# Zero rows of the first attention's stacks: two transfers in place of Pool's clearings, and a wait for each group of weights

## What is computed

```
c_q = x @ w_dq.T;   q_c = (c_q @ w_uq.T)        # 16 heads x 16
c_kv = x @ w_dkv.T; k_c = (c_kv @ w_uk.T); v = (c_kv @ w_uv.T)
q_r = (c_q @ w_qr.T); k_r = (x @ w_kr.T)        # 16 heads x 64
q_r, k_r = _rope(q_r, k_r, offset=0)
q = concatenate([q_c, q_r]); k = concatenate([k_c, k_r])
attn = softmax(q @ k.T * SCALE + causal mask); out = (attn @ v) @ w_out.T
```

## Time and profile before

| | us |
|---|---|
| median of 3 runs | 918.64 |
| lowest and highest of them | 917.73, 919.67 |
| the profiled execution | 916.41 |
| its span on the core | 914.2 |
| PE busy in the span | 791.1 (87%) |
| DVE busy | 365.2 (40%) |
| ACT busy | 290.5 (32%) |
| Pool busy | 224.3 (25%) |

### The profile page before, as it was taken

How to read it: one execution, slowest core, us unless ns; L and a number is a source line. 1 busy time by engine, 2 the same in 40 slices (tenths; PEclk the granted TensorE clock), 3 DMA queues, 4 the chain that set the end, 5 groups by cost and what they waited for, 6 DMA issues and landing times.

```text
span 914.2 us, 14814 instructions
## 1 busy us (share of the span) xinstructions
PE 791.1 (87%) x5020; PEld 602.4 (66%) x5021; DVE 365.2 (40%) x902; ACT 290.5 (32%) x527; POOL 224.3 (25%) x260
## 2 busy tenths in 40 slices
PE   1989799999989999999955289989887999999990
PEld 0767577877767677777734257767665767777760
DVE  8444154543533312222146386676543422222212
ACT  1102103114233333433223214445453234334321
POOL 8341013333131411221123300011312421221212
PEclk9999899999999999999986789999998999999995
DMA  6963914223962216110221641211301111101004
GB/s 198 409 142 107 315 67 93 59 48 89 360 207 74 70 55 207 40 35 23 63 78 32 177 103 34 56 45 35 142 30 53 58 36 34 34 24 34 29 18 143
DMA packets 47692, 88.19 MB, mean 96 GB/s; under 512 B 8884, under 2 KB 36916, under 8 KB 45524
## 3 DMA queue, kind: packets, MB, share of 16 engines
q1 hardware_dynamic: 36104, 54.56, 21.0%
q0 software_dynamic: 7568, 30.97, 9.3%
q10 hardware_dynamic: 3968, 1.97, 0.8%
HBM read 52.33 MB, written 35.13 MB: 96 GB/s over the span
## 4 chain that ended last, share of the span: by engine, by line
PE 80%; DVE 8%; DMA 6%; issue 2%; ACT 2%; POOL 1%; SPq 0%; ACTq 0%; POOLq 0%; DVEq 0%
PE bank L1380 24%; PE bank L1407 13%; PE bank L880 9%; PE bank L459 4%; PE bank L504 4%; PE bank L1393 4%; PE bank L515 2%; PE bank L449 2%; PE bank L533 2%; PE bank L502 2%; PE bank L576 2%; DMA PTR<-rows_out 2%; DVE stat L324 2%; DVE XN L596 1%; PE bank L550 1%
## 5 line engine op out<-in xcount | busy, mean ns | idle before, releaser
L1380 PE MATMUL bank<-wgu,R 128*128 x736 | 225.4, 459 | 0.4 <-issue 0.3
L1380 PEld LDWEIGHTS bank<-wgu,R 128*128 128x128 f32 x736 | 137.7, 193 | 65.8 <-issue 3.5
L1407 PE MATMUL bank<-R 112*128 (+1 forms) x552 | 127.0, 379 | 1.2 <-ACT R L1429 1.2
L1407 PEld LDWEIGHTS bank<-R 112*128 112x128 f32 (+1 forms) x552 | 104.4, 190 | 22.3 <-issue 1.7
L1445 DVE TENSOR_TENSOR R<-R,bank 128x344 f32<-128x344 f32 x92 | 47.2, 513 | 179.9 <-PE bank L1380 172.2
L647 ACT ACTIVATE PTR<-bank 128x512 f32<-128x512 f32 x144 | 83.5, 597 | 97.7 <-PE bank L504 82.2
L1356 POOL DMA_INDIRECT rows_out<-R,XN x46 | 46.0, 999 | 169.4 <-ACT R L1437 157.7
L1452 DVE COPY R<-bank 112x512 f32<-112x512 f32 x46 | 31.7, 690 | 103.7 <-PE bank L1393 103.7
L596 DVE TENSOR_REDUCE XN<-bank 128x2 f32<-128x512 f32 x96 | 63.1, 684 | 10.7 <-PE bank L459 10.7
L1423 ACT ACTIVATE R<-bank 128x344 f32<-128x344 f32 x92 | 41.9, 457 | 76.4 <-PE bank L1380 76.2
L1437 ACT ACTIVATE R<-bank 128x256 f32<-128x256 f32 x46 | 17.7, 384 | 146.7 <-PE bank L1407 146.7
(11 more groups left out here) (167 smaller groups left out, 1292.0 us busy)
## 6 DMA issues: line engine op xcount, KB each, us to landing
wgu<-in_wgu SPq DMA_DIRECT2D x10, 1376.0 KB, 11.4
slots_in<-PTR POOLq DMA_DIRECT2D x1, 9088.0 KB, 26.1
row_of_slot<-in_unused POOLq DMA_DIRECT2D x2, 4544.0 KB, 17.6
R<-slots_in SPq DMA_DIRECT2D x46, 128.0 KB, 2.0
wgu<-R SPq DMA_DIRECT2D x32, 128.0 KB, 2.4
R<-R SPq DMA_DIRECT2D x32, 128.0 KB, 2.4
PTR<-rows_out SPq DMA_DIRECT2D x16, 256.0 KB, 3.1
R<-in_wd SPq DMA_DIRECT2D x8, 448.0 KB, 5.8
```

The source lines that it names most:

```text
L1380: last = nc.tensor.matmul(BK[2 * half + gu][:, 0:IH], xsT[:, p, kk, :], wgu[:, bass.ds(e * (KD * GU) + (kk * GU + gu * I + half * IH), IH) ...
L1407: last = nc.tensor.matmul(down_bank(i)[:, 0:D], hT[0:CH[c], p, c, :], wd[0:CH[c], bass.ds(e * (6 * D) + c * D, D)], start=c == 0, stop=c == 5)
```

## The change

The clearings of the stacks by Pool go. In their place Pool issues two transfers (one for each pair of stacks) that copy zeros from PTR into rows 16 to 31; rows 0 to 15 are no longer cleared, since the placements write them. Pool issues them when wuq, wuk and wuv have landed (s_wu), waits until both have landed (s_slots), waits for wqr and woa, and then issues the fill. SP waits for the two transfers in place of Pool's clearings before it places. The single wait of PE for six weights becomes three: wkr before items 2 to 5, the three of s_wu before 6 to 8, wqr and woa before 9 to 12. Two pairs of x loads share a semaphore each, so DVE waits for both loads of a pair.

```diff
-        s_x = [sem(f"s_x{b}") for b in range(B)]
+        s_x = [sem("s_x01"), sem("s_x23")]
+        s_wk = sem("s_wk")
+        s_wu = sem("s_wu")
...
-        INIT = 5
+        INIT = 3
...
-            for dst, src in ((wkr, "wkr"), (wuq, "wuq"), (wuk, "wuk"), (wuv, "wuv"), (wqr, "wqr"), (woa, "woa")):
+            sp.dma_start(wkr, dr["wkr"]).then_inc(s_wk, 16)
+            for dst, src in ((wuq, "wuq"), (wuk, "wuk"), (wuv, "wuv")):
+                sp.dma_start(dst, dr[src]).then_inc(s_wu, 16)
+            for dst, src in ((wqr, "wqr"), (woa, "woa")):
                 sp.dma_start(dst, dr[src]).then_inc(s_wc, 16)
-            sp.wait_ge(s_init, INIT)
+            sp.wait_ge(s_slots, 16 * 2)
...
-            pool.memset(R1[0:32, 0:2 * HA * S], 0.0).then_inc(s_init, 1)
-            pool.memset(room(EVEN, 2 * HA * S)[0:32, :], 0.0).then_inc(s_init, 1)
             pool.wait_ge(s_init, INIT)
-            pool.wait_ge(s_wc, 16 * 6)
+            pool.wait_ge(s_wu, 16 * 3)
+            for st in (room(EVEN, 2 * HA * S), R1[:, 0:2 * HA * S]):
+                pool.dma_start(st[16:32, :].rearrange("p (n m) -> p n m", n=4),
+                               zeros[0:16, None, 0:2048].broadcast_to([16, 4, 2048])).then_inc(s_slots, 16)
+            pool.wait_ge(s_slots, 16 * 2)
+            pool.wait_ge(s_wc, 16 * 2)
...
-            norm_vector(0, lambda b: (s_x[b], 16))
+            norm_vector(0, lambda b: (s_x[b // 2], 16 * 2))
...
-            pe.wait_ge(s_wc, 16 * 6)
-            project_a_tensor(0, range(2, ITEMS))
+            pe.wait_ge(s_wk, 16)
+            project_a_tensor(0, range(2, 6))
+            pe.wait_ge(s_wu, 16 * 3)
+            project_a_tensor(0, range(6, 9))
+            pe.wait_ge(s_wc, 16 * 2)
+            project_a_tensor(0, range(9, ITEMS))
```

More of the change, by code:

```diff
@@ L645, in exps_scalar @@
                 if i == 0 and n == 0 and l == 0:
-                    nc.scalar.wait_ge(s_slots, 16)
+                    nc.scalar.wait_ge(s_slots, 16 * 3)
                 nc.scalar.activation(PT[:, g % 2, i, :], banks(l, g, True)[i][:, :], ACT.Exp, scale=scale).then_inc(s["exps"], 1)
@@ L1317, in scatter_gpsimd @@
             if b == 0 and l == 1:
-                nc.gpsimd.wait_ge(s_slots, 16)
+                nc.gpsimd.wait_ge(s_slots, 16 * 3)
             both = [(t, slot[:, k * NT + t:k * NT + t + 1], ids[:, k * NT + t:k * NT + t + ROW])
@@ L1611, in _ @@
             for t in range(0, NT, 2):
-                sp.dma_start(xres[:, t:t + 2, :], xd[:, t:t + 2, :]).then_inc(s_x[t // 2], 16)
+                sp.dma_start(xres[:, t:t + 2, :], xd[:, t:t + 2, :]).then_inc(s_x[t // 4], 16)
             for dst, src in ((ident[:, :], "ident"), (identb[:, :].bitcast(U16), "identb"), (masks[:, :, :].bitcast(U16), "masks"),
```

## The result

The changed kernel takes 928.88 us (median of 4 runs, 928.07 to 930.28) against 918.58 us for the kernel before beside it (median of 4, 917.73 to 919.67): a ratio of 1.0118, with a 95% interval of 1.0092 to 1.0144. So it is 10.3 us slower; 927.5 was predicted. Its profiled execution took 928.6 us with a span of 926.8, which is 12.6 us more than the span before.

A forecast was written before the change was run, and what follows sets the result against it. Two chains meeting at PE's first scores, DVE's stall and the placements behind the fill, end within 0.1 us; the second binds. 6.4 + 2.6 = 9.0 us on 916.4 gives 925.4, with the median 2.2 above: 927.5, range 916 to 932.

The forecast's parts named there:

- The first chain: Pool's clearings stall DVE and so PE's first instruction; freed, PE starts near 8.4 against 19.35, costed at zero.
- The waits by group: PE's separate waits for groups of weights cost nothing and give PE up to 3 us more room; zero on the path.
- The zero rows: Pool's two zero transfers, issued at 17.2, move 1.05 MB at 102 GB/s and land at 29.2.
- The quick rival: Zero transfers run at 432 GB/s and land at 21.3; the kernel takes 917 to 920 us; chance 0.12.
- The fill: Pool's fill of slots_in, issued at 29.9 instead of 20.59, its end 1 us later for more placements beside it; lands near 57.
- The placements: SP's 32 placements of batch 0: 11 issued under the fill, 21 left, the last moving 6.4 us to 70.9.
- the third: Placement pace recovers at 45.4 + 9.3 + 1 = 55.7, against a fill landing near 57.
- The rivals with a normal issue, landings late or not: Placements beside the fill issue at 0.64 us: normal landings, 913.3 us, chance 0.12; issue at 0.61, late landings, 918 to 921, 0.10.
- The clock: PE stands several us before its first scores, so their first group runs at 1.2 GHz: 2.6 us more.
- The sum: Last placement's delay plus the low clock: 6.4 + 2.6 = 9.0 us.
- the further 0.06 above the range: Chance of a time above 916 to 932, where the placement pace under a longer fill falls further.
- That the whole delay goes through: Rest of batch 1, second fill and expert weights wait for this work in the same order, so all 9.0 us count.

The follow-up runs named there:

- e1: The kernel before, Pool's clearings kept, with only PE's waits by weight group and the paired x loads: 918.69 us against 918.79, ratio 0.999.
- e3: The changed kernel with ACT's copies clearing rows 0 to 31 instead of the two zero transfers, fill issued once weights landed: 918.73 us against 918.79 before.
- e7: The changed kernel with zero transfers writing rows 0 to 31 instead of 16 to 31, twice the bytes: 930.17 us, ratio 1.0148 to the kernel before.
- e9: The changed kernel plus fourteen unread matmuls between batch 1's projections and the first scores: 922.08 us, ratio 1.005 to the kernel before; changed kernel again 929.76.
- e11: The kernel before, with the fill of row_of_slot issued only after batch 1's placements have landed: 909.66 us against 918.91, ratio 0.9914.
- e6: The changed kernel with ACT clearing instead of zero transfers, slots_in fill after batch 0's placements, row_of_slot fill after batch 1's: 901.79 us against 917.43 before.
- e2: The changed kernel, but Pool doesn't wait for the zero rows before the fill; only SP waits: 925.84 us, ratio 1.0068 to the kernel before.
- e8: The changed kernel plus ten unread matmuls between batch 1's projections and the first scores: 924.43 us, ratio 1.0052 to the kernel before.

## Why the prediction was right, and which terms were off

**The first chain.** Right. The stall was Pool's clearing (e1, which keeps the clearings, keeps PE's start at 19.35), the change frees it, PE starts at 8.01 (8.4 predicted), and it is worth nothing as long as the placements bind (e3). The Trainium skill, "SBUF — State Buffer", section "SBUF: two separate sides", says that a GpSimd operation and those VectorE operations that use the port pair the two share take it as an exclusive lock, held for a whole instruction; the trace agrees, with 6.72 us against 0.17 and an end within 0.03 us of the clearing's.

**The waits by group.** Right at zero (e1).

**The zero rows.** Landed at 30.80, predicted 29.2. Two thirds of the miss are the weights, which landed 1.1 us later than before (wuv at 17.60 against 16.5); the rest is the rate, 92 GB/s in the row against the 102 taken. The value was taken from the 32-row placement by halving, and e7 bears this scaling out. The quick rival, landing at 21.3, is out.

**The fill.** Issued at 31.09 (29.9), landed at 58.89 (57): 27.8 us after issue, 1.7 more than before, where 1 was priced.

**The placements, the term that was mis-sized.** +6.4 us were predicted and +9.1 measured (last one landed at 73.58 against 64.47). The pace came back at 59.72, not 55.7, and 13 had been issued by then, not 11. Worked out from these: the fill's issue moved 1.2 us further than predicted and the fill ran 0.7 longer; the step that failed is the third, that the pace returns 1.3 us before the fill lands, as it had before. Here it returned 0.8 us after, which is 2.1 us; two more placements issued give back 1.3. Together 2.7, the miss. The rivals with a normal issue, landings late or not, are out: 1.61 us at the median against 0.64.

**The clock.** 2.6 predicted; 5.93 − 3.06 = 2.9 in the trace, and 2.8 by e9. The 1.1 us that e9 gains at batch 1 were not foreseen; why the lower clock lasts less long there no run tells.

**The sum.** The prediction has 9.0 us; the scores of batch 1 come 12.0 us later (120.04 against 108.02) and the span is 12.6 longer. The medians moved by 10.3 only, because the profiled execution of before lay 2.2 us below its median and that of after (928.6) on it. So that the forecast of 927.5 came so near to 928.88 is in part luck: both terms were somewhat too small, 3.0 us together, and the offset of the median, which the prediction carried over from before to after, made up for 1.9 of it. The chances given to the forecast and its three rivals already add up to 1.00, so the further 0.06 above the range had no room.

**That the whole delay goes through** held for the changed kernel (12.0 at batch 1, 12.6 at the end), but not as a rule: e9's scores start 7.9 us after those of before (74.10 against 66.23), the attention's first output product comes 6.6 later (132.01 against 125.44), and its time is 3.2 longer, its span 4.7. How much of what is lost between these is more than the difference between two executions isn't shown.

## What to carry to other kernels

Two chains that end within 0.1 us of each other make a repair of one worthless, and what the repair adds to the other counts in full: look for the chain that ends next before you price a stall that goes. A large transfer that nobody needs soon, issued in front of small ones that somebody waits for, was the dearest thing in this start; moving one brought 9.3 us here (e11), and moving two, with the stalled engine freed as well, 15.6 (e6), where freeing the engine alone brought none (e3). No run moved the fill of slots_in alone, with DVE's stall kept; since the two chains end within 0.1 us of each other, little is to be expected of it. A transfer's length goes by the rows (partitions) that it covers as well as by its bytes (e7), so clear a narrow strip by an engine that is idle (ACT took 7.3 us for a pair of stacks in e3) or keep the transfer away from what is queued behind it.

## What was not expected of the hardware

- Beside the fill not only the landing of a placement is late (13.8 us against 2.3) but SP's issue itself takes 1.6 us against 0.64, so SP is on the path. It isn't so beside every fill: beside that of row_of_slot eight placements took 0.61 us each to issue and were only late to land (rows 10). The Trainium skill, "DMA: Bandwidth & Descriptors", section "Queues, rings and completion order", says that each DMA engine takes turns between its rings packet by packet; the late landings agree with shared engines, and no run here shows the turns themselves or why the issue is slower.
- The DMA engines read as busy for 0.86 of the time while the zero rows moved at 92 GB/s, and for 1.02 while the fill of the kernel before moved at 432 (rows 7). A busy share near 1 doesn't tell that much is moved.
- A fill issued 8.9 us earlier behind the zero rows lands only 1.7 us earlier (e2): 35.0 us instead of 27.8.
- Fourteen unread matmuls, 6.8 us of PE's work put into a stand, made the kernel 7.7 us faster by the medians (e9), and ten of them brought nearly as much (e8). The first groups of scores of the two batches behind them account for 3.9 us of e9's gain. The rest, 1.5 us by the ratios and 3.8 by the medians, has no known place; two traces of one program differ by as much (3.7 us, behind the scores of batch 1).
